# Spectral layer and attention convolution: last statistics sums directly behind the row transform, mode weights in 2 KB pieces, one operand block by DMA

## The reference

```
x = x + L0(gn(x));  x = x + L1(gn(x))       # gn: mean and variance per (b, c) image
L0: rfft2, keep 32 x 32 modes, per mode  blk[b,o] = sum_i x_ft[b,i] * w[i,o]  (w real),
    inverse transform, then a 32 x 32 channel matrix fc_w and bias fc_b
L1: att[b] = softmax(sigmoid(mean(x) @ ksm_w.T)) over 16 kernels; kernel = sum_k att * dft_weight[k];
    3 x 3 inverse DFT, clip, grouped 3 x 3 convolution with it, bias, scale
```

## Time and profile before

| what | value |
|---|---|
| median of 3 runs | 147.77 us (147.33 to 148.44) |
| profiled execution, its own time | 147.89 us |
| its span, first to last instruction | 146.1 us |
| outside the span | 1.8 us |
| busy in the span: PE, PEld, DVE, ACT, POOL | 125.8, 91.6, 78.3, 68.2, 44.5 us |
| mean granted TensorE clock | 0.976 |
| chain of waits by engine: PE, ACT, DVE, issue | 62%, 13%, 12%, 7% |

### The profile page before, as it was taken

One profiled execution on the slowest core, in us unless ns is written; L12 is line 12 of the kernel. 1 busy time (PEld: TensorE's weight loads), 2 busy tenths in 40 slices (PEclk: granted clock), 3 DMA queues, 4 the chain that ended last, 5 costly groups with the idle time before them and its releaser, 6 DMA issues.

```text
span 146.1 us, 4992 instructions
## 1 busy us (share of the span) xinstructions
PE 125.8 (86%) x2172; PEld 91.6 (63%) x2172; DVE 78.3 (54%) x194; ACT 68.2 (47%) x134; POOL 44.5 (30%) x40
## 2 busy tenths in 40 slices
PE   0899999594996479899999979997999999999970
PEld 0889998594986369799999968932234322333310
DVE  0089679358758944633378468995751842201220
ACT  0575754519999415513347751499720560111010
POOL 7980000007999999999300000000000000000000
PEclk9999999999599869999999999999999999999999
DMA  4999989996000388868705977295898106563384
GB/s 97 273 265 238 242 216 408 416 416 246 5 0 9 78 179 186 194 152 191 174 12 114 173 141 155 62 176 80 174 170 185 24 18 145 129 144 71 89 177 99
DMA packets 68837, 23.09 MB, mean 158 GB/s; under 512 B 67408, under 2 KB 67664, under 8 KB 68304
## 3 DMA queue, kind: packets, MB, share of 16 engines
q1 hardware_dynamic: 68816, 22.78, 64.7%
HBM read 14.38 MB, written 4.19 MB: 127 GB/s over the span
## 4 chain that ended last, share of the span: by engine, by line
PE 62%; ACT 13%; DVE 12%; issue 7%; DMA 2%; SPq 1%; ACTq 0%; DVEq 0%
PE slot L953 21%; PE slot L807 10%; PE slot L883 10%; PE slot L896 7%; PE slot L872 4%; ACT bd_buf L449 3%; PE slot L830 2%; DMA x_buf<-x 2%; PE slot L863 2%; ACT r_buf L449 2%; ACT conv_w L499 2%; ACT q_buf L476 2%; ACT x_buf L449 2%; DVE y_buf L641 2%; DVE conv_w L728 2%
## 5 line engine op out<-in xcount | busy, mean ns | idle before, releaser
L953 PE MATMUL slot<-w_buf,conv_w 128*32 128x512 f32 x192 | 42.3, 593 | 0.0
L953 PE MATMUL slot<-y_buf,conv_w 128*32 128x512 f32 x192 | 42.2, 593 | 0.0
L953 PEld LDWEIGHTS slot<-w_buf,conv_w 128*32 128x32 f32 x192 | 12.1, 109 | 22.1 <-issue 21.9
L807 PE MATMUL slot<-cst,x_buf 128*64 128x64 f32 x512 | 18.8, 238 | 4.8 <-DMA x_buf<-x 4.2
L807 PEld LDWEIGHTS slot<-cst,x_buf 128*64 128x64 f32 x512 | 18.1, 152 | 5.0 <-issue 5.0
L752 DVE TENSOR_SCALAR bd_buf<-slot,st 128x512 f32<-128x512 f32 x8 | 6.0, 748 | 19.9 <-PE slot L953 19.9
L896 PE MATMUL slot<-cst,t_buf 128*128 128x128 f32 x128 | 15.5, 278 | 0.8 <-issue 0.8
L896 PEld LDWEIGHTS slot<-cst,t_buf 128*128 128x128 f32 x128 | 14.7, 192 | 1.4 <-issue 1.2
L883 PE MATMUL slot<-cst,r_buf 128*64 128x128 f32 x256 | 14.6, 274 | 0.7 <-ACT r_buf L461 0.7
L883 PEld LDWEIGHTS slot<-cst,r_buf 128*64 128x64 f32 x256 | 13.9, 137 | 1.0 <-ACT r_buf L461 0.9
L552 DVE TENSOR_REDUCE row_sq<-q_buf 128x16 f32<-128x1024 f32 (+1 forms) x9 | 9.8, 1098 | 7.8 <-ACT q_buf L431 7.7
(11 more groups left out here) (115 smaller groups left out, 188.5 us busy)
## 6 DMA issues: line engine op xcount, KB each, us to landing
x_buf<-x SPq DMA_DIRECT2D x16, 256.0 KB, 4.1
w_buf<-w_modes SPq DMA_DIRECT2D x4, 1024.0 KB, 9.8
x_buf<-x SPq DMA_DIRECT2D x32, 128.0 KB, 3.3
w_buf<-y_buf SPq DMA_DIRECT2D x16, 256.0 KB, 5.6
out<-bd_buf SPq DMA_DIRECT2D x28, 128.0 KB, 2.8
t_buf<-dft_w SPq DMA_DIRECT2D x1, 1152.0 KB, 14.2
out<-bd_buf SPq DMA_DIRECT2D x8, 64.0 KB, 1.9
cst<-consts SPq DMA_DIRECT2D x1, 388.0 KB, 9.0
```

The lines of the kernel that those rows point to most:

```text
L807: last = pe.matmul(ps[64 * ri:64 * ri + 64, col:col + 64], x_part(k)[:, i, q, :], const("fwd_h")[:, 64 * ri:64 * ri + 64], start=True, sto ...
L953: last = pe.matmul(ps[32 * j:32 * j + 32, 512 * half:512 * half + 512], cw[r][:, b, kw, :], src[:, b, u:u + 8, kw:kw + W], start=(kw == 0) ...
```

## The change

Five edits. (1) PE's list: `f1(7)`, `sums(2)` and `sums(3)` follow `f1(6)` directly, all remaining pairs of k = 0 and k = 1 come after them, and `mix(0)` goes between `f2(2)` and `f2(3)`. (2) `zn` has eight buffers in place of two, in the upper half of `t_buf`, and `operand(n)` no longer waits for ACT. (3) The fourth block (partitions 96 to 127) of each operand is moved by one DMA per k of 32 rows of 4 KB, issued on ACT's queue ahead of the copies of the block with xx = 1, in place of two ACT copies; `mix(k)` and DVE's `copy_t(4)` wait for it. (4) `w_modes` is stored so that each 1 MB part is read in 2 KB pieces, four per partition, in place of one of 8 KB. (5) DVE: `pick(2)` comes behind `copy_y(7)`; the copies of the products of `mix(0)` to `mix(2)` come ahead of `fc_diag` and `bconst`.

```
-        zn = [t_buf[:, at:at + 512].rearrange(...) for at in (2304, 2816)]
+        zn = [t_buf[:, 4096 + 512 * n:4608 + 512 * n].rearrange(...) for n in range(8)]
...
+        bd_moved = [sem(f"bd_moved{k}") for k in range(4)]
...
-                sp.dma_start(modes[:, ml].rearrange("p n xo -> p (n xo)"), w_modes[:, ml]).then_inc(modes_in[ml], 16)
+                sp.dma_start(modes[:, ml].rearrange("p (q n) xo -> p q (n xo)", q=4), w_modes[ml].rearrange("q p n -> p q n")
+                             ).then_inc(modes_in[ml], 16)
...
-                for g in range(1, 4):
+                if xx:
+                    act.dma_start(bd[k][96:128, 3].rearrange("p x n b r -> p (x n b r)"),
+                                  t_buf[96:128, 4096 + 1024 * k:5120 + 1024 * k]).then_inc(bd_moved[k], 16)
+                for g in range(1, 3):
                     ps = slice(32 * g, 32 * g + 32)
-                    ins = act.activation(bd[k][ps, g, xx], zn[n % 2][ps], ACT.Copy)
+                    ins = act.activation(bd[k][ps, g, xx], zn[n][ps], ACT.Copy)
...
-                if k in (3, 5, 6):
-                    pick(k // 2 - 1 if k < 6 else 2)
+                if k in (3, 5):
+                    pick(k // 2 - 1)
...
             copy_y(7)
+            pick(2)
             pick(3)
...
-                if n >= 2:
-                    v.wait_ge(bd_act, n - 1)
-                nc.vector.tensor_tensor(zn[n % 2], z, rstd, ALU.mult).then_inc(zn_ready, 1)
+                nc.vector.tensor_tensor(zn[n], z, rstd, ALU.mult).then_inc(zn_ready, 1)
...
+            for ml in range(3):
+                copy_mixed(ml, 0)
+                copy_mixed(ml, 1)
             v.wait_ge(cst_in, 16)
...
-            for ml in range(4):
+            copy_mixed(3, 1)
...
+                if k == 4:
+                    for moved in bd_moved:
+                        v.wait_ge(moved, 16)
...
                 pe.wait_ge(bd_act, 2 * (ml + 1))
+                pe.wait_ge(bd_moved[ml], 16)
...
             f1(6)
+            f1(7)
             sums(2)
-            pair(0, 2)
-            f1(7)
-            for s in range(3):
-                pair(1, s)
             sums(3)
-            pair(0, 3)
-            pair(1, 3)
+            for k in range(2):
+                for s in range(2 - 2 * k, 4):
+                    pair(k, s)
             f2(2)
+            mix(0)
             f2(3)
-            for ml in range(4):
+            for ml in range(1, 4):
                 mix(ml)
```

More of the change, by code:

```diff
@@ L157, in spectral_then_attention_conv @@
               for t in (bd_buf[:], r_buf[:], x_buf[:, 0:4096], x_buf[:, 4096:8192])]
-        zn = [t_buf[:, at:at + 512].rearrange("p (n b r) -> p n b r", n=M1, b=B) for at in (2304, 2816)]
+        zn = [t_buf[:, 4096 + 512 * n:4608 + 512 * n].rearrange("p (n b r) -> p n b r", n=M1, b=B) for n in range(8)]
         ost = bd_buf[:, 0:2048].rearrange("p (s n) -> p s n", s=2)
@@ L606, in _, with copy_mixed @@
                 operand(n)
+            def copy_mixed(ml, xx):
+                v.wait_ge(mix_done, 2 * ml + xx + 1)
+                nc.vector.tensor_copy(*mixed_part(ml, xx)).then_inc(mixed_dve, 1)
+            for ml in range(3):
+                copy_mixed(ml, 0)
+                copy_mixed(ml, 1)
             v.wait_ge(cst_in, 16)
@@ L1050 @@
                              array("L1_conv_bias").reshape(C, 1), scale.reshape(C, 1), np.tile(scale, (C, 1))], axis=1)
-    modes = array("L0_conv_weight")[0].reshape(C, C, 4, 2, 4, M1).transpose(2, 0, 4, 5, 3, 1).reshape(128, 4, 2048)
+    modes = array("L0_conv_weight")[0].reshape(C, C, 4, 2, 4, M1).transpose(2, 0, 4, 5, 3, 1)
+    modes = modes.reshape(128, 4, 4, 512).transpose(1, 2, 0, 3)
     arrays = {"x": array("x"), "w_modes": np.ascontiguousarray(modes), "dft_w": array("L1_conv_dft_weight"),
```

## The result

| kernel | median | ratio to the kernel before, 95% interval |
|---|---|---|
| before | 147.55 us (4 runs) | 1 |
| changed | 151.51 us (149.81 to 153.18, 4 runs) | 1.0237 (1.018 to 1.0294) |
| changed, measured again later | 149.09 us (148.86 to 150.11, 4 runs) | 1.0179 (1.0125 to 1.0233) |

The change makes the kernel slower, by 2.4% in the first measurement and 1.8% in the second; both are clear of noise, but neither interval says whether it is more or less than 2%. I had forecast 145.1 us. The profiled execution took 151.11 us, its span is 149.3 us, 3.2 more than before. Medians are of all executions, ratios leave out the slow ones (over 1.5% above the fastest of their kernel), and two profiled executions were slow: that of "changed, 8 KB, f2(3) first" and that of "before + first mode part held", from which nothing is read.

The account below looks back on a forecast made before the run. PE's chain of waits was taken as the bound, with code blocks pacing the mixes. `fc` at 51.3 in place of 54.06, 2.75 us earlier, gave 147.89 − 2.75 = 145.1 us; forecast range 143.7 to 146.3, chance 0.45.

Parts of the forecast that it names:

- the third item of part 2: Before `mix(0)`: new DMA issued at 30.9 lands 3.2 us later, at 34.1, the last thing `mix(0)` needs.
- the term for the load: In the new DMA's landing time: 0.4 us added to a quiet store's 2.8 for the mode weights still loading.
- My bound: Upper limit for the new DMA's landing: 5.9 us, a quiet 2.8 plus the 3.15 added to a code packet.
- Rival 3: New DMA queues behind the weights until `dft_w` ends: `mix(0)` at 38.5, `fc` at 55.7, 149.4 us; chance 0.14.
- Sums 3.45 us earlier: End of row transform: last sums follow directly, so the first operand starts at 28.5 in place of 31.96.
- 2 KB pieces shorten a code packet's wait: Before `mix(0)`: PE's code block, entered at 28.1, arrives after 4.2 us, at 32.3, in place of the old 6.58 us.
- rival 1: 2 KB pieces don't help; `mix(0)` late by code or DMA, `fc` 52.6 to 54.0, 146.5 to 147.8 us; chance 0.27.
- Code blocks set the pace of the mixes: From `mix(0)` to `fc`: each 128-record mix is one code block, round trip 3.6 us against 2.33 of matmuls.
- Rival 2: Code never limits the mixes: `mix(0)` at 34.1, 6.4 us won, 141.5 us; chance 0.14.
- `f2(3)` behind `mix(0)` has cover: Column transform's last part gives DVE its last banks near 39.5 and 40.5, four code blocks of slack before `mix(3)`.
- The lower clock before `mix(0)` is covered: `mix(0)` at lower clock, after PE stands still, takes 3.38 us, under the 4.2 of a code block.

Follow-up runs that it names:

- changed, 8 KB, f2(3) first: Changed kernel with mode weights in 8 KB pieces and the last column transform ahead of the first mix; 147.06 us, ratio 0.9984 to the kernel before.
- before + first mode part held: Kernel before, with the first mode part issued only when the first half of f1(5) is done; 148.25 us, ratio 1.0016.
- second profile: The same changed kernel profiled once more, nothing altered; this execution 149.16 us, median of that measurement 149.09 us, ratio 1.0179.
- first profile: Profile of the changed kernel's first measurement; this execution 151.11 us, median 151.51 us, ratio 1.0237.
- the split ones: 2 KB pieces with each mode part as four 256 KB DMAs: in the changed kernel 150.32 us (1.0174), in the kernel before 147.21 us (0.997).

## Why the prediction was wrong

The step that failed is the third item of part 2, the landing of the new DMA. I took 3.2 us from its issue, 2.8 as in a quiet queue and 0.4 for the load, with 5.9 as the bound, "it has 32 rows of 4 KB, so little of its own to move". Issued at 31.25 as forecast (30.9), it took 6.52 us, and 7.1 with 8 KB pieces; issued when the loads were nearly over, 3.0. So the term for the load, which I put at 0.4, measured 3.5. How little a DMA has to move says nothing of how long it waits for its first packet: 3.9 us in place of 1.2. My bound had that wait about right, from a code packet (3.15 us more than in a quiet queue), and lacked the slower rest, 2.6 us in place of 1.8. The late landing moved `mix(0)` from 34.1 to 38.0. The rest of the working then holds: from `mix(0)` to `fc` I had 17.2 us, measured 17.35 (second profile) and 17.0 (8 KB), so `fc` came at 55.4 in place of 51.3 and the time at 149.1 in place of 145.1. Rival 3 had this time (149.4, deciding from a landing 6.0 us after the issue), and I gave it 0.14. Its mechanism held only in part: the DMA didn't wait for the end of `dft_w`, which landed at 40.3 in the second profile, but got its packets from 35.14 on. What rival 3 lacked for a larger chance was the comparison I could have made: the code packet asked for at 28.83, in the same loads, was usable only 6.6 us later. That was the nearest row for any transfer issued there on another queue, and I read only the added 3.15 us from it.

Point by point:
- *Sums 3.45 us earlier*: right, where no code block is late (28.95 and 28.88 against 28.5, so 3.0 us). In the first profile the new gap of 2.64 us took it, a packet that my sum had at the old wait. I had looked at the gaps behind the last sums, not at the block in the row transform whose packet started at 20.4, just as the mode parts arrived.
- *2 KB pieces shorten a code packet's wait*: wrong, rival 1 was right. Asked for near 23 and 29 us, the packets started 3.6 and 4.2 us later before, 4.0 and 4.3 in the changed kernel with 8 KB, and 3.9 and 3.6 with 2 KB in the second profile. For the shorter wait I had leaned on the Trainium skill, "DMA: Bandwidth & Descriptors", section "Queues, rings and completion order", by which an engine changes between queues after each packet. A fourth of the piece gave no shorter wait here. By rival 1's sum the time would have been 146.5 to 147.8; it left out that the pieces alone make the kernel before 2.15% slower, and why they do isn't settled.
- *Code blocks set the pace of the mixes*: right, and the best part. Gaps of 1.5 us at 127 records, round trips of 3.5 to 4.1 us against my 3.6. Rival 2 is out, and doubling two mixes cost 8.7 us. The Trainium skill, "Runtime: NRT & Kernel Launch", section "Instruction fetch mechanics", calls the cost of crossing a block "mostly hidden". In this kernel it isn't. At full clock, DVE and ACT had slack in the mixes; ACT's saved copies, the purpose of the DMA, were worth nothing here.
- *`f2(3)` behind `mix(0)` has cover*: wrong with the late DMA, where it costs 1.5 us of `fc`.
- *The lower clock before `mix(0)` is covered*: right. In the second profile `mix(0)` ran at 0.50 of the clock for the whole of its 3.94 us, and a block took 3.8 in any case. What I left out is that the lower clock can fall on `fc` (8.7 to 9.3 in place of 7.4 us in four of the profiles), by which single executions differ by 1.5 to 2 us.

In the first profile the two costs overlap: `zn` late by the code gap, the DMA issued at 33.92, nearer to the end of the loads, took 4.4 us. There the mixes took 18.65 us with blocks 4.0 us apart (32.36 is followed by 38.92, 42.91, 46.75, 50.75, 54.76); each packet there started 1.6 to 1.8 us after its block was entered, in place of the 1.1 that I had counted on, and why is open.

## What to carry to other kernels

A small transfer that replaces compute is worth its landing time at the moment of its issue, not its size: look up what a transfer on another queue needed in the same load, from request to use, and take that whole. When PE's gaps have no releaser, count the instructions between them; if they are a constant number apart, the stage is bound by the arrival of code, and neither faster helpers nor a better order of the list gives anything beyond that pace. A block asked for in the middle of a burst of loads comes later still (3.3 to 4.5 us to its packet here, in place of 1.1). Put work that needs nothing ahead of a wait, not behind it.

## What was not expected of the hardware

The same DMA of 128 KB, on-chip memory to on-chip memory, took 3.0 us when issued at 34.7 us and 6.5 to 7.1 us when issued at 31.2 us, amid the loads. Code packets took about as long to start behind 2 KB pieces (3.3 to 4.3 us over the profiles used, without the split ones) as behind 8 KB ones (3.6 to 4.5 us). With little else in the DMA queues, the wait before a code packet lay between 1.0 and 1.8 us, in one and the same execution, for no cause that the traces show; 1.6 to 1.8 throughout goes with the slow mixes of the first profile.
